# Where layer norms stand beside attention: a placing rule of their own, and a separate step for spreading reciprocals

## What is computed

```python
h = _ln(x, ln1_w, ln1_b) * (1 + sc1[:, None, :]) + sh1[:, None, :]
q, k, v = jnp.split(h @ Wqkv + bqkv, 3, axis=-1)
x = x + _attn(q, k, v) @ Wos + bos
h = _ln(x, ln2_w, ln2_b) * (1 + sc2[:, None, :]) + sh2[:, None, :]
x = x + _attn(h @ Wq + bq, context @ Wk + bk, context @ Wv + bv) @ Woc + boc
h = _ln(x, ln3_w, ln3_b) * (1 + sc3[:, None, :]) + sh3[:, None, :]
x = x + jax.nn.gelu(h @ W1 + b1, approximate=False) @ W2 + b2
```

## Time and profile before

| | us |
|---|---|
| median of the runs | 4615.15 |
| profiled execution | 4592.06 |
| its span, first to last instruction | 4590.2 |
| TensorE matmul busy | 4082.9 (89%) |
| VectorE busy | 3092.3 (67%) |
| ScalarE busy | 2079.0 (45%) |
| POOL busy | 1347.2 (29%) |

### The profile page before, as it was taken

How to read it: one execution, slowest core, us unless ns; L and a number is a source line. 1 busy time by engine, 2 the same in 40 slices (tenths; PEclk the granted TensorE clock), 3 DMA queues, 4 the chain that set the end, 5 groups by cost and what they waited for, 6 DMA issues and landing times.

```text
span 4590.2 us, 56559 instructions
## 1 busy us (share of the span) xinstructions
PE 4082.9 (89%) x20828; PEld 2498.1 (54%) x20828; DVE 3092.3 (67%) x4625; ACT 2079.0 (45%) x3756; POOL 1347.2 (29%) x664
## 2 busy tenths in 40 slices
PE   7999989789998887998999977888999999987889
PEld 5343356634334675555555545666555555546668
DVE  5888855688885666777777854455677677774355
ACT  2555644355565443444444435553344444434541
POOL 1100011100000124655555543421344444441120
PEclk7999989999998998999999988998999999998999
DMA  4223231123223332233222324423322222216420
GB/s 129 40 42 49 44 58 35 43 30 56 41 29 55 57 61 65 64 65 66 61 63 63 65 51 109 97 70 70 69 65 65 66 65 65 58 39 153 95 62 19
DMA packets 158515, 286.64 MB, mean 62 GB/s; under 512 B 36458, under 2 KB 70052, under 8 KB 157216
## 3 DMA queue, kind: packets, MB, share of 16 engines
q1 hardware_dynamic: 158240, 283.03, 29.6%
HBM read 105.01 MB, written 29.64 MB: 29 GB/s over the span
## 4 chain that ended last, share of the span: by engine, by line
PE 61%; DVE 16%; issue 6%; ACT 5%; POOL 5%; SPq 4%; DMA 2%; DVEq 0%; POOLq 0%; ACTq 0%
PE PS L993 26%; PE PS L1173 12%; PE PS L1069 4%; PE PS L1215 4%; PE PS L1065 4%; PE PS L1303 3%; DVE t L1733 3%; PE PS L1225 2%; DVE t L1729 2%; SPq L2179 1%; POOL t L1997 1%; SPq L2162 1%; DVE PS L1818 1%; POOL t L2024 1%; POOL t L2011 1%
## 5 line engine op out<-in xcount | busy, mean ns | idle before, releaser
L993 PE MATMUL PS<-t 128*128 128x512 f32 (+4 forms) x7896 | 1983.8, 382 | 152.6 <-ACT t L1446 30.4
L1446 ACT ACTIVATE t<-PS 128x512 f32<-128x512 f32 (+2 forms) x1600 | 1165.4, 749 | 1107.8 <-PE PS L993 1101.8
L993 PEld LDWEIGHTS PS<-t 128*128 128x128 f32 (+2 forms) x7896 | 1242.5, 186 | 700.5 <-issue 256.7
L1173 PE MATMUL PS<-t 128*32 128x512 f32 (+2 forms) x4352 | 812.3, 612 | 0.2
L1729 DVE TENSOR_REDUCE t<-PS 128x1 fp32r<-128x1024 f32 x512 | 621.4, 1219 | 267.9 <-PE PS L1065 261.0
L1733 DVE TENSOR_REDUCE t<-PS 128x1 f32<-128x512 f32 x1024 | 649.3, 682 | 72.4 <-PE PS L1069 70.8
L2024 POOL TENSOR_TENSOR t<-t 128x1024 f32<-128x1024 f32 x256 | 618.0, 2414 | 125.8 <-ACT t L1446 99.1
L1069 PE MATMUL PS<-t 96*128 96x512 bf16 x1024 | 372.4, 396 | 31.0 <-DVE t L1733 13.2
L1065 PE MATMUL PS<-t 128*128 128x512 f32 x1024 | 336.8, 411 | 46.0 <-DVE t L1729 26.8
L2020 POOL TENSOR_TENSOR t<-t 128x1024 f32<-128x1024 f32 x64 | 156.1, 2439 | 744.4 <-PE PS L1183 468.2
L1961 POOL TENSOR_TENSOR t<-t 128x2048 f32<-128x2048 f32 x24 | 109.5, 4564 | 833.0 <-DMA t<-in_rows 564.6
(11 more groups left out here) (134 smaller groups left out, 3950.0 us busy)
## 6 DMA issues: line engine op xcount, KB each, us to landing
t<-t SPq DMA_DIRECT2D x256, 256.0 KB, 3.9
t<-t SPq DMA_DIRECT2D x512, 128.0 KB, 3.7
t<-scr_n SPq DMA_DIRECT2D x288, 128.0 KB, 6.3
scr_n<-t SPq DMA_DIRECT2D x72, 256.0 KB, 2.2
t<-t SPq DMA_DIRECT2D x256, 64.0 KB, 2.1
t<-in_L_Wg SPq DMA_DIRECT2D x16, 768.0 KB, 4.6
t<-in_L_W SPq DMA_DIRECT2D x36, 256.0 KB, 3.2
t<-in_L_Wo SPq DMA_DIRECT2D x64, 128.0 KB, 2.7
```

The source lines that it names most:

```text
L993: ins = e.matmul(out, l, r, start=i == 0, stop=i == len(terms) - 1, tile_position=tp)
L1173: ins = e.matmul(banks[S.ot][wd * j:wd * j + wd, :], u.v[j][kt], P[0:S.pr, j, :], start=kt == 0, stop=kt == S.nkt - 1, tile_position=(0, w ...
L1446: e.activation(dst, src, ACT.Exp, scale=S.L.scale).then_inc(*expd.inc((S.i, i)))
```

## The change

Three things change, all in the places of steps. A function `norm_put` replaces `norm_steps` in the attention stages: statistics come closer together, the root stands at 0.26 of the window, each quarter takes a seventh of the window from 0.3 on, its turn stands 0.65 of a quarter's pace behind its second row and its split 0.65 behind the turn, so that the next quarter's rows stand before the split. The windows stay, but for the narrow cross stage's own second half, 0.9 to 3 in place of 1.1 to 2.6; there the second half's projections move 0.35 later and two stacks 0.1 and 0.2 later. And the ScalarE spread, until now a part of `sums16`, becomes the step `spread16` with a place of its own in the tail. TensorE's and VectorE's parts of `sums16` stay where they are.

```diff
+    def norm_put(plan, p, lo, hi):
+
+        w = hi - lo
+        for t in range(8):
+            plan.put(lo + 0.03 * w * t, 0, [("ln_stats", p, t)])
+        plan.put(lo + 0.26 * w, 0, [("ln_rstd", p)])
+        at, pace = lo + 0.3 * w, 0.7 * w / 4.9
+        for q in range(4):
+            for t in range(2):
+                plan.put(at + pace * (q + 0.2 * t), 0, [("ln_norm", p, 2 * q + t)])
+            plan.put(at + pace * (q + 0.85), 0, [("ln_turn", p, q)])
+            plan.put(at + pace * (q + 1.5), 0, [("ln_split", p, q)])
+        plan.put(hi, 0, [("ln_bias", p)])
...
-        tail = (0.2, 0.7, 1.2, 1.45) if S.cross else (0.07, 0.4, 0.53, 0.72)
+        tail = (0.2, 0.45, 0.7, 1.2, 1.45) if S.cross else (0.07, 0.25, 0.4, 0.53, 0.72)
...
-                    todo = [("sums16", S, an), ("norm", S, an), ("proj", S, an, 0), ("proj", S, an, 1)]
+                    todo = [("sums16", S, an), ("spread16", S, an), ("norm", S, an), ("proj", S, an, 0), ("proj", S, an, 1)]
...
-                    plan.put(1.1, 2.6, norm_steps(nxt))
-                    plan.put(10.4, 13.5, norm_steps(last))
+                    norm_put(plan, nxt, 0.9, 3)
+                    norm_put(plan, last, 10.4, 13.5)
...
-                            at = (-3, 2.7)[b] + 0.8 * ch
+                            at = (-3, 3.05)[b] + 0.8 * ch
...
-                        plan.put((-1.95, -1.95, 0.05, 0.05, 4.4, 4.4, 6, 8)[g], 0, [("stack16", S, g)])
+                        plan.put((-1.95, -1.95, 0.05, 0.05, 4.5, 4.6, 6, 8)[g], 0, [("stack16", S, g)])
...
-                    plan.put(0.1, 2.3, norm_steps(nxt))
-                    plan.put(9.2, 12.6, norm_steps(last))
+                    norm_put(plan, nxt, 0.1, 2.3)
+                    norm_put(plan, last, 9.2, 12.6)
...
-                    plan.put(6.75, 9.2, norm_steps(nxt))
-                    plan.put(23.8, 30, norm_steps(S.parts[1].next))
+                    norm_put(plan, nxt, 6.75, 9.2)
+                    norm_put(plan, S.parts[1].next, 23.8, 30)
...
-                    plan.put(10.0, 12.4, norm_steps(nxt))
+                    norm_put(plan, nxt, 10.0, 12.4)
...
-                    plan.put(26.05, 30, norm_steps(last))
+                    norm_put(plan, last, 26.05, 30)
...
-            elif what == "sums16":
+            elif what == "spread16":
```

## The result

The changed kernel takes 4597.65 us (median of 7 runs, 4587.71 to 4600.65), the kernel before 4610.93 in the same comparison (7 runs, 4605.56 to 4621.1). The ratio is 0.9972, 95% interval 0.996 to 0.9984: 13 us faster. I had predicted 4593, 22 us under the median then known. The kernel before was run beside the experiments 74 more times; its medians there were 4602 to 4611.

A forecast was written before the change was run, and what follows sets the result against it. TensorE carries 61% of the chain; its turns idled 73.8 us, 69.9 of it waiting for VectorE's normalising. Gains of 33.9 us less costs of 11.8 gave net 22 us, from 4615 to 4593 us; range 4568 to 4624.

The forecast's parts named there:

- Narrow cross, second half: Second half's norm in narrow cross attention: first turn's wait stays, later waits shrink; gain 2.3 us a layer, 4.6 us.
- Mlp's norm: Norm of the following mlp, in narrow cross attention: 3.3 of 4.3 us of waits go, twice, gain 6.6 us.
- Wide self, second half: Second half's norm in wide self attention: 2 of 5.1 us of turn waits go, twice, gain 4 us.
- Wide cross: Norms in wide cross attention: gain 2.7 us in layer 2 and 4 in layer 3, sum 6.7 us.
- Narrow self: Four norms in narrow self attention: nothing to win; 1 us of cost for all, from statistics coming closer together.
- Late wide norms: The four late norms of the wide stages: nothing to win, sharing the 1 us cost written for all.
- The clock: TensorE's lower clock level beside the norms partly goes: 5 us each narrow layer, 2 us for the wide ones, 12 us.
- The spread: ScalarE's spread of reciprocals as its own step: worth nothing in plain units, no new wait for TensorE.
- The rows of the maxima: Narrow cross: moved projections lengthen TensorE's 4.1 us wait for these rows to 6 to 8; cost 3.3 us a layer, 6.6.
- Rival 2: Slower: row DMAs behind the stacks cost 5 us a layer, 4625 us; sign, rows' wait above 9 us; chance 0.14.
- The bias: POOL's bias add holds VectorE's cast at most 4.1 us instead of 2.7; cost 1.4 us in three norms, 4.2 us.
- Rival 1: VectorE takes the turn wait's place; only mlp's norms and wide cross gain: 4614 us; chance 0.17, including turns waiting as before.

The follow-up runs named there:

- the early weights: Changed kernel with one weight load and POOL's weight split of the wide self attention placed 0.4 and 0.5 units earlier: 4579.85 us, ratio 0.995 to the kernel before.
- the old placing: Changed kernel with only the norm of the wide self attention's second half again spread evenly over its window: 4579.05 us, ratio 0.9953 to the kernel before.
- the late bias: Changed kernel with POOL's bias add also waiting for the norm's last split: 4585.16 us, ratio 0.9944; the same line in the kernel before: 4603.98 us, 0.9992.
- Kernels 9 and 12: Changed kernel (9) and kernel before (12), each with bias add after last split, second stack at 5.2, earlier weight load and split: 4563.1 and 4604.34 us.
- the kernel with the later stack: Changed kernel with the second stack of the narrow cross attention's second half moved from 4.6 to 5.2: 4582.52 us, ratio 0.9953 to the kernel before.

## Why the prediction came out right, and where it was wrong

The time, 4597.65, lies 5 us from the forecast, but some terms were wrong and cancelled, so that much of the nearness is luck. In the order of the prediction:

- *Narrow cross, second half, 2.3 us a layer.* The first turn's wait stayed (3.6 forecast, 4.8 measured) and the other three went, as said. The stretch up to cross 4 gained 3.4 and 4.4 us, its part of the clock term and the bias's hold within it, but by another way than I had said. The new wait of 5.7 us behind the held cast takes the place of those that went, and what fell is TensorE's busy time, from 51.3 to 47.7 us in layer 0, at a granted clock of 0.84 in place of 0.77. I had halved the price for a VectorE that would become the bound. Its busy time from 618.9 to 636.2 us did rise, from 9.18 to 14.05 of 17.3 us, but some 3.5 us of that are the hold itself.
- *Mlp's norm, 3.3 us a layer.* The turns' wait fell from 4.3 to 1.6 and 2.0 us, the stretch by 3.2 and 4.3. Right for the waits. In layer 0 TensorE's busy time did not change (41.9 us), so there it is gaps alone; in layer 1 it fell from 42.0 to 39.2, so there the clock is the larger part.
- *Wide self, second half, a gain of 2 us a layer.* Wrong in sign: it cost 5.7 and 4.8 us. The turns' 5.1 us went as said. The step that failed is the sentence "After, one row stands behind that weight split instead": I saw one hold of the port pair and put no price on it. With three of the norm's instructions now standing in a row, each met one of POOL's. That the holds are the cause is shown by the early weights (8.9 and 7.7 us back) and by the old placing (5.7 and 4.8). Their price is not fixed: with the same holds and the same waits layer 2 lost 5.7 us in the trace of after and 1.1 in that with the late bias, the difference being the granted clock.
- *Wide cross, 2.7 and 4 us.* Layer 2 gained 2.4 in units 6 to 10 and gave back 2.6 in units 10 to 19, so the term came to nothing. The turns' waits fell from 7.0 to 3.4 us, as meant, but that for POOL's product, which was to stay, grew from 6.8 to 9.1, and one for the split from 1.1 to 2.6:

```profile
PE PS L1111 <- POOL t L2025: 9.1, 3, 7.9
PE PS L1028 <- DVE t L1633: 3.4, 2, 2.8
PE PS L1007 <- DVE t L1646: 2.6, 1, 2.6
```

  Both are the clock: TensorE's busy time is 2.6 us less in the first (granted clock 0.87 for 0.81) and 2.7 more in the second. Units 10 to 19 take 110.6 or 110.7 us in six traces, old places and new, and 113.2 to 113.6 in eight. Layer 3 lost 2.4: the add at 4243.98 held the subtraction for 4.87 us, as shown above. With the late bias the same units take 42.1 us, 3.4 less than before: the 4 us of gain were there, and the hold took 5.8.
- *Narrow self, "nothing to win", 1 us of cost for all.* Too little. Units 9 to 12 take 2.8 us more in layer 0 (91.0 to 92.7 in all seven traces with the new places there, 89.4 to 89.9 in the seven without) and 1.2 more in layer 1. In layer 0 the waits for the maxima's reductions grew from 0.6 to 1.7 us, and unit 9 to 10 ran at a granted clock of 0.95 in place of 1.00.
- *Late wide norms, "nothing to win".* Wrong: 4 to 5 us less in each layer in every kernel that has the new places (167.5 to 168.2 against 171.8 to 173.3 in layer 2), 9.4 us in all. I had looked at the turns' waits alone, and there are none. By the table of that stretch TensorE's busy time fell too. Before, then after:

```profile
2561.90:2704.60 142.70, 133.31 (x554) 69.31 (x556) 110.34 (x119) 63.41 (x110) 77.46 (x32) 0.99 0.20 42
...
2567.20:2704.90 137.70, 131.56 (x554) 68.83 (x556) 107.72 (x118) 63.44 (x109) 77.12 (x32) 1.00 0.20 43
```

  Of the 5.0 us, 1.75 are TensorE's busy time, the rest gaps; which instruction made them is open.
- *The clock, 12 us.* In the narrow cross stages it came near to what I had sized. Full clock missing over the same units, self 15 to cross 5 and cross 8 to 13: 17.3 + 8.4 us before and 15.6 + 6.9 after in layer 0 (0.78 and 0.83, then 0.80 and 0.85), 17.4 + 8.4 and 13.3 + 3.6 in layer 1 (0.78 and 0.83, then 0.83 and 0.92). That is 3.2 and 8.9 us less, 5 and 5 predicted. In the wide self units it went the other way:

```profile
2079.90:2212.40 132.50, 117.25 (x498) 67.72 (x500) 104.12 (x110) 55.87 (x90) 76.59 (x34) 0.96 0.27 58
...
2075.90:2214.20 138.30, 120.81 (x498) 70.77 (x500) 107.29 (x110) 55.83 (x90) 76.05 (x34) 0.93 0.26 56
```

  that is 5.3 us missing before and 9.7 after, where I had a gain of 2. Over the whole kernel the median clock of the runs went from 0.9485 to 0.950, some 7 us at full clock. The kernels of after with one or more repairs ran at 0.9515 to 0.956.
- *The spread, nothing.* Right by itself, 1.0001; but the narrow cross norm's gain came only together with it, an interaction that I had not considered.
- *The rows of the maxima, 3.3 us a layer.* The wait grew to 5.5 and 5.4 us, a little under the 6 to 8 forecast; cross 4 to 5 grew by 2.5 and 3.4 us. Right in direction; the stretch itself scatters by nearly 4 us. Rival 2's bound of 9 us was not reached.
- *The bias, 1.4 us in each of three norms.* The cast was held 4.2 us (4.63 less 0.42), as its bound said. By the difference of 13 and 4 the change made it cost 9 us more, against 4.2, but uncertain by some 11. TensorE stood still 5.7 and 5.6 us for it in the narrow layers, where taking it away only moved the hold, and 5.8 in layer 3, where the units took 5.8 us less without it. By the rule of the Trainium skill, "SBUF — State Buffer", section "SBUF: two separate sides", the hold would last POOL's whole instruction. The trace agrees: 4.63 us beside an add of 4.51.

By the stretches, the clock within them, the gains are 7.8 (narrow norm) + 7.5 (mlp's) + 9.4 (late wide) = 25 us, the costs 10.5 (wide self) + 5.9 (rows) + 2.4 (layer 3's wide cross) + 4.0 (narrow self) = 23; 2 us are left, where I had 22 and the runs of the whole kernel say 13, with an interval of 7 to 18. The attention stages as a whole are even 2.8 us longer in the trace of after. So these two executions do not account for the 13 us; the one of before was some 19 us under the median of its runs. Kernels 9 and 12 show the change's worth more clearly, 41 us by the traces and 45 by the runs. Rival 1 would have given 4614 and rival 2 4625; neither came. The forecast was near because 9 us that I did not see made up for part of a wide self term that was off by 14 (from plus 4 to minus 10), a wide cross term off by 9 and a narrow self term off by 3. What the signs to look for said: the wait for line 1619 came to 34 us and not under 30; rival 1's sign, waits for the reductions of the maxima, did appear, in the wide self units because of POOL, and with 1.7 us in layer 0's self attention.

## What to carry to other kernels

When a step list is reordered on an engine that shares its SBUF port pair with another, put the other engine's instructions beside the new order one by one: here each two-input addition, cast or scaling that fell into one of them lasted until that one ended, and a hold of 2 to 5 us ahead of something that TensorE awaits is as large as the wait that the reordering removes. Look for such holds in the durations of one line, and check that a repair changed the wait it was meant for: the 4.6 us that the late bias seemed to give in layer 2's self attention were the clock's. A wait of 87 us on an engine off the path was worth nothing that could be measured, and one of 1.2 us on TensorE was in one place followed by 10 us at half clock. Repairs and reorderings do not add: try the repairs on the old order as well before deciding what made the gain.

## What the runs showed of the hardware

- A held VectorE instruction is recorded as long, not as waiting: 128 x 32 elements took 4.56 us beside POOL's add of 4.50, 0.22 us otherwise. VectorE's reduction out of PSUM at 2105.36, beside POOL's split begun at 2105.52, kept its 1.22 us. In the whole trace of after 258 of the 512 reductions at that line start while a POOL instruction has over 0.2 us to go, and none took more than 1.23 us; so did 34 of the 192 statistics at line 1618, none over 0.43. All 27 casts and subtractions of the norms (lines 1644 and 1646) that start so took longer than alone. The reductions:

```profile
L1743 DVE TENSOR_REDUCE t<-PS x512: 1172/1224/1227, 1750.2 to 4087.8; 128x1 fp32r<-128x1024 f32 x171
```

- SP's queue made late what stood behind a long group of reads. With six of twelve stack reads (2.76 us of issue) moved behind the four rows, the wait for the rows fell from 5.5 to 0.2 us, and the load behind them was issued 5.6 us after the rows in place of 2.9 (679.21 and 673.59; 671.24 and 668.36).
- The clock did not answer equal waits equally. In wide self units 9 to 13 of layer 2 the same waits of TensorE came with 0.93 and 138.3 us in the trace of after and 0.96 and 133.7 us in that with the late bias. In the kernel with the later stack TensorE waited 1.18 and 0.50 us in layer 0 and was granted 0.50 for the 10 us after; in layer 1 it waited 0.92 and 0.78 us at the same instructions, with the same busy time in 8 us (6.29 against 6.32), and stayed at full clock. What decides is open. The table by stretch of layer 1:

```profile
1500.00:1508.00 8.00, 6.29 (x57) 4.15 (x55) 5.16 (x15) 2.79 (x4) 1.27 (x1) 1.00 1.09 160
1508.00:1518.00 10.00, 9.94 (x89) 6.76 (x88) 6.80 (x16) 4.65 (x6) 1.27 (x1) 1.00 0.71 138
```
